# An adaLN block with gated linear attention and an fp4 feed-forward: batch 0's front is split, small operations change their engine, and the order tables are written anew

## The reference, cut to what matters

```python
mod = (silu(c) @ wmod).reshape(4, 6, 1, 128)        # sa, ca, ga, sb, cb, gb
ga, gb = sign(ga) * max(|ga|, 0.25), sign(gb) * max(|gb|, 0.25)
h = layernorm(x) * (1 + ca) + sa                     # x: (4, 1024, 128)
# attention without softmax, 16 heads of 8 columns
q, k = l2norm(h @ Wq), l2norm(h @ Wk);  v = h @ Wv
beta, fast, slow = sigmoid(h @ Wb), sigmoid(h @ Wfd + bfd), sigmoid(h @ Wsd + bsd)
k_beta = k * beta
hmid = silu(k_beta @ Wtf1 + btf1)                    # 4 values per head and row
flux = clip(sigmoid(hmid @ Wtf2 + btf2), 0.01, 0.99)
w_f, w_s = exp(suffix sums of log(fast)), exp(suffix sums of log(slow))
M_f, M_s = (k_beta * w)^T (v * beta) / (sum w + 1e-6) # an 8x8 matrix per head
o = alpha * q M_f + (1 - alpha) * q M_s;  alpha = 0.5 + 0.3 * flux
x = x + ga * (o @ Wo)
h = layernorm(x) * (1 + cb) + sb
x = x + gb * fp4_ffn(h)      # silu(gate) * up, width 352; inputs and weights in fp4, blocks of 16
```

## Time and profile before

| | |
|---|---|
| median of 3 runs | 222.32 us (221.98 to 222.64) |
| the profiled execution | 222.68 us, span of its instructions 220.9 us |
| busy | PE 185.0, PEld 131.6, DVE 178.0, ACT 143.8, POOL 155.8 us |
| mean granted TensorE clock | 0.992 |

### The profile page before, as it was taken

One profiled execution on the slowest core, in us unless ns is written; L12 is line 12 of the kernel. 1 busy time (PEld: TensorE's weight loads), 2 busy tenths in 40 slices (PEclk: granted clock), 3 DMA queues, 4 the chain that ended last, 5 costly groups with the idle time before them and its releaser, 6 DMA issues. The chain is left out here.

```text
span 220.9 us, 3435 instructions
## 1 busy us (share of the span) xinstructions
PE 185.0 (84%) x924; PEld 131.6 (60%) x924; DVE 178.0 (81%) x432; ACT 143.8 (65%) x328; POOL 155.8 (71%) x183
## 2 busy tenths in 40 slices
PE   0789939798999979498897989799799898978983
PEld 0434405363767647365764967577779495764873
DVE  3647998888598959999999998988998887876730
ACT  2057898999999797954594365466356477364541
POOL 7330306697998999599897998778669868774540
PEclk9999996999999999999999999999999999999999
DMA  6690000000000000000000000000000000001011
GB/s 184 167 253 2 0 0 1 0 3 0 1 0 1 0 4 0 0 0 0 4 24 0 0 27 25 1 24 4 0 24 24 24 27 24 3 25 49 0 47 50
DMA packets 11355, 5.66 MB, mean 26 GB/s; under 512 B 1668, under 2 KB 11208, under 8 KB 11336
## 3 DMA queue, kind: packets, MB, share of 16 engines
q1 hardware_dynamic: 11024, 5.31, 8.6%
q10 hardware_dynamic: 312, 0.13, 0.2%
HBM read 3.34 MB, written 2.10 MB: 25 GB/s over the span
## 5 line engine op out<-in xcount | busy, mean ns | idle before, releaser
L458 POOL TENSOR_TENSOR q_r<-q_x,q_rs 128x960 f32<-128x960 f32 (+2 forms) x18 | 29.8, 1653 | 14.8 <-DVE q_rs L927 14.6
L1048 PE MATMUL pa<-wcat,hT 128*128 128x496 f32 x64 | 33.1, 650 | 3.2 <-ACT sq L581 2.0
L470 POOL TENSOR_TENSOR q_o<-q_r,q_sp 128x960 f32<-128x960 f32 (+2 forms) x18 | 29.6, 1645 | 8.1 <-DVE q_r L938 7.5
L1118 PE MATMUL pa<-guT,hqT 128*128 128x352 f32 x64 | 25.4, 478 | 4.0 <-ACT hqT L665 3.7
L1141 PE MATMUL pa<-wdg,fqT 128*128 128x128 f32 x192 | 26.7, 275 | 0.0
L1120 PE MATMUL pv<-guT,hqT 128*128 128x352 f32 x64 | 24.5, 464 | 0.0
L1141 PEld LDWEIGHTS pa<-wdg,fqT 128*128 128x128 f32 x192 | 24.0, 192 | 0.0
L674 ACT ACTIVATE sgl<-pa 128x352 f32<-128x352 f32 x32 | 14.3, 462 | 13.1 <-PE pa L1118 9.4
L659 ACT ACTIVATE q_A<-q_r 128x960 f32<-128x960 bf16 (+2 forms) x18 | 15.9, 884 | 9.8 <-POOL q_r L458 6.6
L1048 PEld LDWEIGHTS pa<-wcat,hT 128*128 128x128 f32 x64 | 12.2, 208 | 15.6 <-issue 6.4
L935 DVE SCALAR_TENSOR_TENSOR q_x<-q_A,q_r 128x960 f32<-128x960 f32 (+2 forms) x18 | 18.5, 1030 | 3.4 <-ACT q_A L659 3.3
(11 more groups left out here) (150 smaller groups left out, 454.0 us busy)
## 6 DMA issues: line engine op xcount, KB each, us to landing
out_dram<-x_all SPq DMA_DIRECT2D x16, 128.0 KB, 1.8
...
```

What stands on the lines that cost most here:

```text
L458: g.tensor_tensor(blocks(q_r[:, s % 2, c]), blocks(q_x[:, s % 2, c]), spread(q_rs[:, s % 2, n]), ALU.mult)\
L470: g.tensor_tensor(blocks(q_o[:, s % 2, c]), blocks(q_r[:, s % 2, c]), spread(q_sp[:, s % 2, n]), ALU.mult)\
L1048: te.matmul(bank_a(("PP%d" % k, i))[:, 0:NCAT], hT[:, b, 2 * j + k, :], wcat[:, :], start=True, stop=True).then_inc(S["a_full"], 1)
L1118: te.matmul(bank_a(("G%d" % k, i))[:, 0:I], lhs, guT[:, 0, :], start=True, stop=True)\
```

## The change

- **Front.** `wmod` is loaded in two parts: the 256 columns for `colmod` first, the other 512 after batch 1's x. ACT loads c, Wtf1, Wk, Wq in this order. GpSimd writes only what the front needs (`ident`, `rep8`, `mask`, `mhalf`), then `wraw`'s zeros; the rest is a step `KC` after P0:2, and GA:0 and GC:0 wait for it. `setup` is cut into steps CT, RP, CM, WK, WQ, which wait for their own inputs alone.
- **Statistics.** P0:0 goes in two halves of four tiles, on VectorE and in GpSimd's power. `nmr` is formed only for batches 2 and 3, which use it.
- **Columns.** `colmod` is copied by ScalarE (two activations of 4 columns) out of `pa`, not by VectorE out of `pg`.
- **Bias.** ScalarE's halving of `btf2` stands in GE:0 rather than in the front.
- **Flux.** GpSimd's addition of `btf1` is gone: ScalarE's Silu is four instructions of 128 columns each, one for each of the 4 values of a head, with the bias as a per-partition operand. GpSimd's product with `Wtf2` is gone: VectorE forms the sum as one scaled copy and three multiply-and-add instructions of 128 columns, each of which waits for the one before.
- **Order.** All four tables are written anew.

```diff
@@ the order tables, first lines of two of the four @@
-        setup:0 KW:0 PX:0 PX:1 PX:2 PP:0 PP:1 PX:3 PP:2 PX:4 PP:3 PX:5 MB:0 PX:6 XN:8 PP:4 PP:5 GA:0 XN:9 PX:7
+        CT:0 CM:0 WK:0 WQ:0 PX:0 PX:1 KW:0 PX:2 PP:0 PX:3 PP:1 PX:4 PP:2 PX:5 PP:3 PX:6 XN:8 MB:0 PX:7 XN:9 PP:4
-        P0:0 MV:0 XN:0 XN:1 XN:2 XN:3 P0:1 PP:0 XN:4 XN:5 PP:1 P0:2 PP:2 XN:6 GA:0 P0:3 PP:3 W0:0 GB:0 XN:7 GK:0
+        P0:0 XN:0 XN:1 MV:0 SB:0 XN:2 P0:1 XN:3 XN:4 PP:0 XN:5 XN:6 P0:2 PP:1 PP:2 XN:7 GA:0 PP:3 P0:3 W0:0 GB:0
...
+        def stat_spans(b):
+
+            return [slice(0, T // 2), slice(T // 2, T)] if b == 0 else [slice(0, T)]
+
+        def stat_count(b, k):
+            return k + 1 if b == 0 else b + 2
...
-            sp.dma_start(wmod_sb[:, :], wmod).then_inc(S["wmod"], 16)
+            sp.dma_start(wmod_sb[:, 0:2 * D], wmod[:, 0:2 * D]).then_inc(S["wmod0"], 16)
...
             sp.dma_start(x_all[:, 1], x_v[1]).then_inc(S["x1"], 16)
+            sp.dma_start(wmod_sb[:, 2 * D:6 * D], wmod[:, 2 * D:6 * D]).then_inc(S["wmod"], 16)
...
+            def KC(_):
+                g.memset(tri[:, :], 1.0).then_inc(S["pool_c"], 1)
...
             def P0(b):
-                pool.wait_ge(S["const"], N_CONST)
-                pool.wait_ge(S["ve"], b + 1)
-                g.tensor_tensor(rstd[:, b, :], ve[:, b, :], mhalf[:, 0:T], ALU.pow).then_inc(S["rstd"], 1)
-                pool.wait_ge(S["rstd"], b + 1)
-                g.tensor_tensor(nmr[:, b, :], nmean[:, b, :], rstd[:, b, :], ALU.mult).then_inc(S["nmr"], 1)
+                if b == 0:
+                    pool.wait_ge(S["const"], 1)
+                for k, w in enumerate(stat_spans(b)):
+                    pool.wait_ge(S["ve"], stat_count(b, k))
+                    g.tensor_tensor(rstd[:, b, w], ve[:, b, w], mhalf[:, w], ALU.pow).then_inc(S["rstd"], 1)
+                if b >= XN_VECTOR:
+                    pool.wait_ge(S["nmean"], stat_count(b, 0))
+                    pool.wait_ge(S["rstd"], stat_count(b, 0))
+                    g.tensor_tensor(nmr[:, b, :], nmean[:, b, :], rstd[:, b, :], ALU.mult).then_inc(S["nmr"], 1)
...
-                pool.wait_ge(S["hin0"], b + 1)
-                h4 = hin[:, :, :, :].rearrange("p t h j -> p (t h) j")
-                g.tensor_tensor(h4, h4, btf1_b[:, :].unsqueeze(1).to_broadcast([P, T * H, HM]), ALU.add)\
-                    .then_inc(S["hin"], 1)
...
-            def GE(b):
-
-                pool.wait_ge(S["hmid"], b + 1)
-                h4 = hmid[:, :, :, :].rearrange("p t h j -> p (t h) j")
-                g.tensor_tensor(h4, h4, wtf2_b[:, :].unsqueeze(1).to_broadcast([P, T * H, HM]), ALU.mult)\
-                    .then_inc(S["hz0"], 1)
 
...
-            def setup(_):
+            def CT(_):
                 t = bank(("CT", 0))
                 a.activation(scT[:, :], t[:, 0:NB], ACT.Silu).then_inc(S["a_free"], 1)
-                for k, dst in enumerate((wqT, wkT)):
-                    t = bank(("WT%d" % k, 0))
-                    a.activation(dst[:, :], t[:, 0:P], ACT.Copy).then_inc(S["a_free"], 1)
-                act.wait_ge(S["wsm"], 16 * 5)
-                a.activation(btf2_h[:, :], btf2_b[:, :], ACT.Copy, scale=0.5).then_inc(S["btf2h"], 1)
+
+            def WK(_):
+                t = bank(("WT1", 0))
+                a.activation(wkT[:, :], t[:, 0:P], ACT.Copy).then_inc(S["a_free"], 1)
+
+            def CM(_):
+                t = bank(("CM", 0))
+                a.activation(colmod[:, 0, :], t[:, 0:NB], ACT.Copy).then_inc(S["col"], 1)
+                a.activation(colmod[:, 1, :], t[:, NB:2 * NB], ACT.Identity, bias=1.0).then_inc(S["a_free"], 1)
+
+            def WQ(_):
+                t = bank(("WT0", 0))
+                a.activation(wqT[:, :], t[:, 0:P], ACT.Copy).then_inc(S["a_free"], 1)
...
-                act.wait_ge(S["hin"], b + 1)
-                if b >= 1:
-                    act.wait_ge(S["hz0"], b)
+                act.wait_ge(S["hin0"], b + 1)
+                if b >= 1:
+                    act.wait_ge(S["hz"], HM * b)
                 tables(SILU_TABLES)
-                a.activation(hmid[:, :, :, :], hin[:, :, :, :], ACT.Silu).then_inc(S["hmid"], 1)
+                for j in range(HM):
+                    a.activation(hmid[:, :, :, j], hin[:, :, :, j], ACT.Silu, bias=btf1_b[:, j:j + 1]).then_inc(S["hmid"], 1)
 
             def GE(b):
-                act.wait_ge(S["hz"], b + 1)
+                act.wait_ge(S["hz"], HM * (b + 1))
+                if b >= 1:
+                    act.wait_ge(S["al0"], b)
+                else:
+                    act.wait_ge(S["wsm"], 16 * 5)
+                    a.activation(btf2_h[:, :], btf2_b[:, :], ACT.Copy, scale=0.5).then_inc(S["btf2h"], 1)
+                tables(SILU_TABLES)
                 act.wait_ge(S["btf2h"], 1)
-                if b >= 1:
-                    act.wait_ge(S["al0"], b)
-
-                tables(SILU_TABLES)
                 a.activation(yt[:, :, :], hz[:, :, :], ACT.Tanh, scale=0.5, bias=btf2_h[:, 0:1]).then_inc(S["yt"], 1)
...
             def MV(_):
-                dve.wait_ge(S["a_free"], slot_a[("CT", 0)] + 1)
-                v.tensor_copy(scB[:, :, :], scT[:, :].unsqueeze(2).to_broadcast([P, NB, P])).then_inc(S["scB"], 1)
-                dve.wait_ge(S["const"], N_CONST)
+                dve.wait_ge(S["const"], 2)
                 t = gate_bank(("REP", 0))
                 v.tensor_tensor(bd1[:, :, :], mask[:, :, 0:HM], t[:, 0:HM].unsqueeze(1).to_broadcast([P, H, HM]),
                                 ALU.mult).then_inc(S["g_free"], 1)
-                t = gate_bank(("CM", 0))
-                v.tensor_copy(colmod[:, 0, :], t[:, 0:NB]).then_inc(S["col"], 1)
-                v.tensor_scalar(colmod[:, 1, :], t[:, NB:2 * NB], 1.0, None, ALU.add).then_inc(S["g_free"], 1)
+
+            def SB(_):
+                dve.wait_ge(S["a_free"], slot_a[("CT", 0)] + 1)
+                v.tensor_copy(scB[:, :, :], scT[:, :].unsqueeze(2).to_broadcast([P, NB, P])).then_inc(S["scB"], 1)
 
             def XN(i):
 
                 b, j = divmod(i, NP_)
                 if b >= XN_VECTOR:
                     return
-                dve.wait_ge(S["rstd"], b + 1)
+                dve.wait_ge(S["nmean"], stat_count(b, j // 2))
+                dve.wait_ge(S["rstd"], stat_count(b, j // 2))
...
+                for k, w in enumerate(stat_spans(b)):
+                    dve.wait_ge(S["x0b" if k else "x%d" % b], 16)
+                    for t in range(w.start, w.stop):
+                        v.bn_stats(st6[:, r, t, :], x_all[:, b, t, :]).then_inc(S["bn"], 1)
+                    for t in range(w.start, w.stop):
+                        dve.wait_ge(S["bn"], T * b + t + 1)
+                        v.bn_aggr(mv[:, r, t, 0:2], st6[:, r, t, :]).then_inc(S["mv"], 1)
+                    dve.wait_ge(S["mv"], T * b + w.stop)
+                    if b == 0 and k == 0:
+                        dve.wait_ge(S["eps"], 2)
+                    v.tensor_reduce(ve[:, r, w], mv[:, r, w, 1:3], axis=AX.X, op=ALU.add).then_inc(S["ve"], 1)
+                    v.tensor_scalar(nmean[:, r, w], mv[:, r, w, 0], -1.0, None, ALU.mult).then_inc(S["nmean"], 1)
...
-                h4 = hmid[:, :, :, :].rearrange("p t h j -> p (t h) j")
-                dve.wait_ge(S["hz0"], b + 1)
+                dve.wait_ge(S["hmid"], HM * (b + 1))
                 if b >= 1:
                     dve.wait_ge(S["yt"], b)
-                v.tensor_reduce(hz[:, :, :].rearrange("p t h -> p (t h)"), h4, axis=AX.X, op=ALU.add)\
-                    .then_inc(S["hz"], 1)
+                v.tensor_scalar(hz[:, :, :], hmid[:, :, :, 0], wtf2_b[:, 0:1], None, ALU.mult).then_inc(S["hz"], 1)
+                for j in range(1, HM):
+                    dve.wait_ge(S["hz"], HM * b + j)
+                    v.scalar_tensor_tensor(hz[:, :, :], hmid[:, :, :, j], wtf2_b[:, j:j + 1], hz[:, :, :],
+                                           ALU.mult, ALU.add).then_inc(S["hz"], 1)
...
+            def CT(_):
+                pe.wait_ge(S["ident"], 1)
...
+            def CM(_):
+                pe.wait_ge(S["wmod0"], 16)
+                a_done(("CT", 0))
+                t = bank_a(("CM", 0))
...
```

More of the change, by code:

```diff
@@ L248, in adaln_block_kernel @@
         steps = {engine: order(engine) for engine in ORDER}
-        fills_a = {"setup": ["CT", "WT0", "WT1"], "KW": ["KW"], "MB": ["MB%d" % b for b in range(NB)],
+        fills_a = {"CT": ["CT"], "WK": ["WT1"], "CM": ["CM"], "WQ": ["WT0"], "KW": ["KW"], "MB": ["MB%d" % b for b in range(NB)],
                    "W3": ["WT%d" % k for k in range(2, 8)] + ["WD0", "WD1", "WD2"],
@@ L322, in _ @@
             sp.wait_ge(S["out"], 16 * PAIRS)
-        N_CONST = 9
+        N_CONST = 7
         @block.gpsimd
@@ L1016, in MB @@
                 pe.wait_ge(S["scB"], 1)
+                pe.wait_ge(S["wmod"], 16)
                 for b in range(NB):
@@ L1072, in GG @@
             def GG(b):
+                if b == 0:
+                    a_done(("WT0", 0))
```

167 lines of the change are left out of this document (79 added, 88 removed).

## The result

The changed kernel takes **219.94 us** (median of 4; 217.84 to 221.04) against 222.33 for the kernel before in the same runs: **0.9881 of before, 95% interval 0.9847 to 0.9915**, faster by 1.2%. Forecast were 223.0 us, slower by 0.3%. Repeated, it took 219.73 us, 0.9844 (0.980 to 0.9888). Some executions of a kernel are more than 1.5% slower than its fastest; the ratios leave these out, the medians hold them.

The account below looks back on a forecast made before the run. A latency-bound front to 17 us, then ScalarE paces, then VectorE with GpSimd close behind. Terms -0.9 + 0 + 0 + 1.5 + 0.6 - 0.5 = +0.7 gave 223.0 us, range 219.8 to 225.8.

Parts of the forecast that it names:

- the sum behind O2:0: Total: -0.9 at O2:0, flux sum 0, 0 and +1.5 in batches 1 to 3, ScalarE +0.6, GpSimd -0.5: +0.7 us.
- Front, -2.0 at the end of GA:0: Start of the kernel: PP:0 at about 9.9 instead of 12.24, so `lf` of batch 0 done 2.0 us earlier.
- of my cases the best: TensorE's faster pace in the front: gain 2.3 if as much earlier as its work, 1.4 if unmoved, 2.8 if earlier still.
- W1's wait, +1.2: ScalarE's stretch: W1's activation, ahead of GD:0, waits for VectorE, ready at 36.9 with ScalarE there at about 35.7: +1.2 us.
- Wait before wexp gone, -0.8: ScalarE's stretch before O2:0: the wait of 0.78 us ahead of `wexp` disappears, -0.8 us.
- Silu in four, +0.66 a batch: ScalarE's flux activations: four take 1.2 us against 0.54 for one, +0.66 a batch, bounds +0.35 and +1.1.
- O2:0, -0.9: End of ScalarE's stretch, 58.95 us before: -2.0 -1.2 -0.8 +1.2 +1.3 +0.1 +0.5, so O2:0 comes 0.9 us earlier.
- The flux sum, +1.5 a batch: VectorE's four chained flux instructions replace one sum and may wait for GpSimd: +1.5 us a batch, between +0.6 and +2.9.
- ScalarE +0.6: Batches 2 and 3: the four Silus' extra +0.66 a batch is half hidden in ScalarE's idle third, +0.6 us.
- Relief of GpSimd, -0.5: GpSimd loses 2.1 us of work a batch, counted as -0.5 us in all, bounds 0 and -2.5.
- The front's gain lasts: Rival 1, chance 0.32: TensorE paces earlier, no wait at W1, flux products slip between GpSimd's; -2.7 us, 219.6 us.
- Rival 2: VectorE starves at the port, chance 0.15: every multiply-and-add waits for a GpSimd product, +5.4 us, 227.7 us.

Follow-up runs that it names:

- a_order_old: The changed code with its four order tables put back to those of the kernel before: 224.33 us, 1.0084 of the kernel before.
- b_front: The changed kernel's front with the old flux and the old order: 220.94 us, 0.993 of the kernel before.
- d_weights_old: The changed kernel in its new order, flux weights back on GpSimd and one sum on VectorE, bias still in four Silus: 219.32 us, 0.9836 of the kernel before.
- b_flux_new: The kernel before with the new flux alone, old front and old order: 226.44 us, 1.0182 of the kernel before.

## Why the prediction was wrong

**The step that failed is the sum behind O2:0**, "-0.9 + 0 + 0 + 1.5 + 0.6 - 0.5": behind O2:0 it has +1.6 us of flux costs on before's 159.4 and no term for the new tables, where 4.2 us less were measured. The only moves of the tables that it priced (XN:9 and PX:7, W1, M in one piece) stand ahead of O2:0. For the code in the old order the sum holds: in a_order_old the part behind O2:0 takes 160.8 us (58.49 to 219.29), 1.4 more than before. In the new order it fails in two ways that are one interaction: the tables are worth 2.0% with the new flux, more than the whole result and nothing with the old one, and the flux, priced at +3.0 us in all, is a gain of 1.9 us (2.7 by the repeated run).

By step:

- *Front, -2.0 at the end of GA:0.* The place was right and the size was not: `lf` 2.68 us earlier. Predicted for PP:0 were 9.9; it is 9.18. Two powers of 1.02 and 1.12 us (1.04 expected). TensorE's faster pace came with 12.0 us where I took 15.2 (17.5 less 2.3), so of my cases the best, a gain of 2.8, holds. Alone and in the old order the front leads by 2.97 us at O2:0 (b_front, 55.98) and is worth 1.6 us at the end.
- *W1's wait, +1.2.* Did not come: `w_r` was ready at 34.9, two microseconds earlier than 36.9. VectorE began W1 at 31.27, 1.0 earlier than forecast, and needed 3.6 us for it instead of 4.6; most of that is `w_sp`, 0.31 us where it took 1.09 before.
- *Wait before wexp gone, -0.8.* Wrong: it is 1.19 now.
- *Silu in four, +0.66 a batch.* Four take 1.77 us, 0.42 from start to start, so they cost 1.1 more than one: my upper bound.
- *O2:0, -0.9.* -0.72. Two errors cancelled: the front's larger gain and no wait at W1 against dearer Silus and the wait at `wexp`. That the number came out is luck.
- *The flux sum, +1.5 a batch.* Right as a busy time: 9.1 us for 2.7 is +1.6. The Trainium skill's rule (SBUF — State Buffer, Who interferes with whom), that such instructions contend with GpSimd and a sum never does, agrees with rows here: the sum's mean is 685 ns in d_weights_old too, `hz` instructions have means of 534 and 585. What they cost together was under-priced. The forecast sum for the flux (Silus +1.3, bias +0.1, `hz` +1.5, ScalarE +0.6, relief -0.5) is +3.0; in the old order the run says 4.0. Part of the rest is ahead of O2:0, which comes 2.14 us later in b_flux_new (61.09) where 1.4 were forecast.
- *Relief of GpSimd, -0.5.* The bound to -2.5 was the better guess in the new order: with the weights back on GpSimd nothing changed, though VectorE then had 4.0 us less, and with the bias back there too 2.9 us were lost.

The rival nearest in time, "The front's gain lasts" (219.6), was right in TensorE's pace, in the missing wait at W1 and, in the new order, in GpSimd's relief. It wanted O2:0 at -2.6 (-0.72 came) and +0.6 a batch for the flux sum (+1.6 came), and had no term for the tables either, so its time is luck. Rival 2 set its mark at a mean of 0.6 us for an `hz` instruction; at 0.591 the flux alone cost 4.0 us.
